# Routing one chunk ahead in the experts stage, a rebuilt phase scan, and new first instructions in six kinds of stage

## What is computed

```
phi = k_val[..., None] * theta
num_re = cumsum(p_w * cos(phi)); num_im = cumsum(p_w * sin(phi)); den = cumsum(p_w)
out_re = sum(s_re * qr + s_im * qi)       # s = num / den, summed over the 8 frequencies
```

```
probs = softmax(flat @ router_w); weights, indices = top_k(probs, 2); weights /= weights.sum()
h = silu(flat @ wg) * (flat @ wu) * comb[:, :, None]      # comb: one weight per token and expert
out = shared experts + einsum('tem,emd->td', h, wd)
```

## Time and profile before

| | us |
|---|---|
| median of 3 runs (lowest, highest) | 8263.17 (8258.72, 8267.3) |
| the profiled execution, its own time | 8261.89 |
| its span in the profile | 8260.2 |
| `scan`, 4961 to 5591 | 630 |
| `moe`, 5693 to 6337 | 644 |
| `lru`, 6337 to 6559 | 222 |
| `Aatt`, 282 to 1062 | 780 |
| `Catt`, 3169 to 4388 | 1219 |

### The profile page before, as it was taken

The page is one execution under the profiler, slowest core; times in us unless marked ns, Lnnn a source line. Parts: engine busy times, 40 slices in busy tenths (PEclk is TensorE's granted clock), DMA queues, the critical chain, the costliest instruction groups (busy, mean ns, idle before and its releaser), DMA issues. The chain is left out here.

```text
span 8260.2 us, 122768 instructions
## 1 busy us (share of the span) xinstructions
PE 6734.6 (82%) x30724; PEld 3442.2 (42%) x30724; DVE 4886.6 (59%) x12027; ACT 2733.4 (33%) x6003; POOL 1566.9 (19%) x847
## 2 busy tenths in 40 slices
PE   6799958988898866999994486776886689889989
PEld 3233334554465432222223352334443345544554
DVE  3555557634774535777775749994334676337645
ACT  0255524612471101555551113331110146124621
POOL 1111115100510011000000007880000261006100
PEclk9899979999999987999997698998988899999999
DMA  5322244542454274222223221103001345424541
GB/s 177 95 60 59 52 131 146 172 136 73 149 173 146 81 250 115 72 64 66 64 49 105 82 75 41 30 25 114 23 30 32 101 149 169 139 71 138 172 153 55
DMA packets 921871, 833.01 MB, mean 101 GB/s; under 512 B 239752, under 2 KB 786528, under 8 KB 921248
## 3 DMA queue, kind: packets, MB, share of 16 engines
q1 hardware_dynamic: 491920, 505.95, 21.2%
q10 hardware_dynamic: 429568, 323.08, 12.5%
HBM read 486.33 MB, written 345.74 MB: 101 GB/s over the span
## 5 line engine op out<-in xcount | busy, mean ns | idle before, releaser
L1216 ACT ACTIVATE Catt_E<-Catt_t 128x512 f32<-128x512 f32 x1024 | 576.8, 596 | 501.6 <-DVE Catt_t L1179 319.7
L1155 DVE CUSTOM_DVE_ANT_0 Catt_S<-Catt_s,Catt_win 128x1024 f32<-128x1024 f32 x512 | 621.3, 1215 | 40.9 <-DMA Catt_win<-skewed 38.8
L1155 DVE CUSTOM_DVE_ANT_0 Aatt_S<-Aatt_s,Aatt_win 128x128 f32<-128x128 f32 (+7 forms) x512 | 377.2, 756 | 325.7 <-PE Aatt_s L1094 320.0
L1137 PE MATMUL Catt_o<-Catt_E,Catt_V 128*32 128x256 f32 (+1 forms) x3840 | 548.6, 404 | 0.0
L1216 ACT ACTIVATE Aatt_E<-Aatt_t 128x512 f32<-128x512 f32 (+3 forms) x768 | 355.4, 489 | 325.5 <-PE Aatt_t L1119 257.4
L1179 DVE TENSOR_TENSOR Catt_t<-Catt_t,Catt_near 128x256 f32<-128x256 f32 (+2 forms) x640 | 281.2, 456 | 261.6 <-PE Catt_t L1116 229.9
L1116 PE MATMUL Catt_t<-Catt_Q,Catt_K 123*128 123x512 bf16 x1024 | 327.9, 388 | 91.9 <-ACT Catt_E L1216 71.8
L1094 PE MATMUL Catt_s<-Catt_K,Catt_Q 96*128 96x512 bf16 x1024 | 324.4, 400 | 46.8 <-DMA Catt_near<-near_s 38.1
L2304 PE MATMUL scan_cum<-scan_X,scan_after 128*128 128x512 f32 x448 | 251.3, 644 | 121.8 <-DVE scan_pr L2373 117.5
L1137 PE MATMUL Aatt_o<-Aatt_E,Aatt_V 128*32 128x256 f32 (+2 forms) x2304 | 324.5, 389 | 0.0
L2306 PE MATMUL scan_cum<-scan_X,scan_upto 128*128 128x512 f32 x512 | 279.0, 637 | 39.5 <-POOL scan_X L2280 23.5
(11 more groups left out here) (724 smaller groups left out, 15070.5 us busy)
## 6 DMA issues: line engine op xcount, KB each, us to landing
bias_rows<-line SPq DMA_DIRECT2D x16, 960.0 KB
skewed<-bias_win ACTq DMA_DIRECT2D x16, 960.0 KB, 5.9
Catt_win<-skewed SPq DMA_DIRECT2D x16, 960.0 KB, 4.7
rec<-state_in_r ACTq DMA_DIRECT2D x32, 416.0 KB, 2.4
scan_r<-rec SPq DMA_DIRECT2D x64, 208.0 KB
Aatt_Q<-q_parts SPq DMA_DIRECT2D x32, 384.0 KB
Aatt_K<-k_parts SPq DMA_DIRECT2D x32, 384.0 KB
Catt_Q<-q_parts SPq DMA_DIRECT2D x32, 384.0 KB
```

What stands on the lines that cost most here:

```text
L1137: ins = t.matmul(o_ps[f:f + 2 * hd, x:y], V[:, b, kb, h, :], E[:, kb % NB, h, x:y], start=kb == 0, stop=kb == end and y == hi)
L1155: v.tensor_tensor_reduce(out=S[:, j % 2, 0:w], in0=s_ps[j % 2][:, 0:w], in1=win[:, 0 if causal else h, w0:w0 + w], scale=-1.0, scalar=BIG, ...
L1216: a.activation(E[:, kb % NB, h, lo:hi], t_ps[n % 2][:, 0:hi - lo], ACT.Exp, scale=scale).then_inc(exped, 1)
```

## The change

It does six things.

1. `scan`: `ph` goes to PSUM (one buffer) and so do `ys` (two). The whole number is found by two engines: ACT writes `nn = ph + MAGIC` (a new instruction `whole`), DVE writes `f = (nn - MAGIC) - ph` in one instruction; L2357 on DVE and L2275 on POOL go. PE does the sines before the cosines. POOL's weighing now also waits for DVE's. The lags become 0 to 4.
2. `moe`: the chunk after is routed during this one. The logits of chunk c+1 come after group k = 2, `route` on DVE at k = 3, the exponential on ACT at k = 4, `choose` on DVE at k = 5, the transposes on PE at k = 8, and ACT's copy at k = 9. SP then writes `combT` to memory (`c_s`) and reads it back into `cb` [128, 2, 8, 512], each row broadcast over 64 partitions. The `sel` matmuls go; the second multiply reads `cb` from SBUF. The down product waits group by group.
3. `lru`: the tables are made during `enter`, on DVE and ACT, and kept in SBUF to the end.
4. `qkv_rotary`: PE waits for the weights alone, and the first columns are issued ahead of the table.
5. `thin_attention`: Q and K have their own semaphore and are loaded at once; V, `ext` and `near` count on `late_in`; the first window is loaded right after Q and K, the `of` copies after the second batch; DVE sets the ones in K.
6. `local_attention`: V has its own semaphore `V_in`.

```diff
 # stage_state_scan
+            def whole(it, j):                      # ACT
+                n = it * ST + j
+                a.wait_ge(ph_done, n + 1)
+                a.wait_ge(f_done, n + 1)
+                a.activation(nn[:, j % 2, :], ph[:], ACT.Identity, bias=magic[:]).then_inc(rounded, 1)
-            pipelined(a, B, ST, ((0, trig), (3, store)))
+            pipelined(a, B, ST, ((1, trig), (0, whole), (4, store)))
-                    for i in range(2):
+                    for i in (1, 0):               # PE: sines, then cosines
...
+            def fraction(it, j):                   # DVE
+                n = it * ST + j
+                v.wait_ge(rounded, n + 1)
+                v.wait_ge(trig_done, n + 1)
+                v.scalar_tensor_tensor(out=f[:, j % 2, :], in0=nn[:, j % 2, :], scalar=-MAGIC, in1=ph[:],
+                                       op0=ALU.add, op1=ALU.subtract).then_inc(f_done, 1)
             def phase(it, j):
+                v.drain()
                 v.wait_ge(r_in[j % R], it * (ST // R * 16) + (j // R + 1) * 16)
-                v.wait_ge(f_done, n + 1)
-                v.tensor_tensor(khm(ph[:, j % 2, :]), khm(th[...]), r[...], ALU.mult)
-                v.drain()
-                v.tensor_scalar(nn[:, j % 2, :], ph[:, j % 2, :], MAGIC, -MAGIC, ALU.add, ALU.add).then_inc(ph_done, 1)
+                v.tensor_tensor(khm(ph[:]), khm(th[...]), r[...], ALU.mult).then_inc(ph_done, 1)
-            pipelined(v, B, ST, ((0, phase), (1, weigh), (2, read), (3, reduce)))
+            pipelined(v, B, ST, ((1, fraction), (0, phase), (2, weigh), (3, read), (4, reduce)))
-            pipelined(g, B, ST, ((1, weigh), (0, fraction), (2, add)))
+            pipelined(g, B, ST, ((2, weigh), (3, add)))
             def weigh(it, m):                      # POOL
+                g.wait_ge(x_done[1], it * ST + (m + 3))
 # stage_experts
+            def weights(it, c):                    # SP
+                s = c % 2
+                sp.wait_ge(combT_done, it * 2 + (c + 2))
+                sp.dma_start(c_s[s * NE:(s + 1) * NE, :], combT[:, s, :]).then_inc(c_out[s], 16)
+                sp.wait_ge(c_out[s], it * 16 + (c // 2 * 16 + 32))
+                sp.wait_ge(hid_done, it * (2 * NJ) + (c * NJ - NJ + 2 + NJ))
+                rows = c_s[s * NE:(s + 1) * NE, :].rearrange("(j e) t -> e j t", e=2)
+                for e in range(2):
+                    sp.dma_start(cb[e * 64:(e + 1) * 64, s], rows[e:e + 1].to_broadcast([64, NR, CH])).then_inc(cb_in[s], 16)
+            def chunk(it, c, more, ahead):
+                if more:
+                    columns(it, c, ahead)
+                for u in range(c * 4, c * 4 + 4):
+                    tail.load(sp, it, u)
+                if more:
+                    weights(it, c + 1)
...
-                    if j < NR:                     # PE
-                        if j == 0:
-                            t.wait_ge(combT_done, nc_ + 2)
-                        t.wait_ge(hid_done, n + 2)
-                        t.matmul(c_ps[:], sel[:, j * P:(j + 1) * P], combT[:], start=True, stop=True).then_inc(cb_done, 1)
+                    if more and k == 2:
+                        logits(it, c + 1)
+                    if more and k == 8:
+                        turn_weights(it, c + 1)
...
+            def chunk(it, c, more, ahead):         # PE
+                up(it, c, more, ahead)
+                if ahead:
+                    t.wait_ge(silu_done, it * (2 * NJ) + (c + 1) * NJ)
+                    turn(it, c - 1) if c else turn(it - 1, 1)
+                down(it, c)
+            logits(0, 0)
+            turn_weights(0, 0)
+            chunks(t, chunk)                       # 2 chunks unrolled, a loop over 2 batches, 2 unrolled
+            def chunk(it, c, more, ahead):         # DVE
...
+                    ins = v.tensor_tensor(h, sg[:, k % 2, :], u_ps[k % 2][:], ALU.mult)
+                    if j < NR:
+                        v.drain()
+                        if j == 0:
+                            v.wait_ge(cb_in[c], it * 32 + 32)
+                        ins = v.tensor_tensor(h, h, cb[:, c, j, :], ALU.mult)
+                    ins.then_inc(hid_done, 1)
+                    if more and k == 3:
+                        route(it, c + 1)
+                    if more and k == 5:
+                        choose(it, c + 1)
 # stage_enter, with the recurrence's tables (the same instructions as before, in a class)
+            tables.load(sp, logs)
+            columns(0)
+            tables.sines(s)
+            with s.Fori(1, B) as it:
+                columns(it)
+        @block.vector
+        def _(v):
+            tables.make(v)
 # stage_qkv_rotary
+            columns(0, 0)
+            sp.dma_start(rt[:], rot.rearrange("(t p) a d -> p t a d", p=P)).then_inc(r_in, 16)
...
-            t.wait_ge(w_in, 16 * 8)
+            t.wait_ge(w_in, 16)
-            v.wait_ge(w_in, 16 * 8)
+            v.wait_ge(r_in, 16 * 7)
 # stage_thin_attention
-            sp.wait_ge(set_up, 1)
-            t.wait_ge(set_up, 1)                   # now only ahead of the first turned maxima
-                    t.wait_ge(head_in[b], it * (16 * LOADS) + 16 * LOADS)
+                    t.wait_ge(head_in[b], it * 32 + 32)
-            g.memset(K[K0:K0 + PARTS], 1.0)
-            v.wait_ge(set_up, 1)
+            v.memset(K[K0:K0 + PARTS], 1.0).then_inc(K_ones, 1)
+            if causal:
+                v.wait_ge(win_made, 1)
 # stage_local_attention
-                             ).then_inc(head_in[b], 16)
+                             ).then_inc(V_in[b], 16)
```

More of the change, by code:

```diff
@@ L341, in _, with columns @@
                 s.sem_inc(cols_out[i], 16)
-            with s.Fori(0, B) as it:
+            def columns(it):
                 for u in range(NT):
@@ L1014, in load @@
             def load(it, b):
-                if b == 1 and not causal:
+                if b == 1 and not causal and not isinstance(it, int):
                     window(it, 0)
@@ L1172, in add_near @@
                 b, h, kb = i // GS, i % 2, i % GS // 2
+                if i % GS == 0 and not causal:
+                    v.wait_ge(late_in[b], it * (16 * LATE) + 16 * LATE)
                 for c, lo, hi, n, some in units[i]:
@@ L2323, in trig @@
                 a.activation(ab[:], f[:, s, :], ACT.Abs)
[L2324 removed]
+                a.activation(sn[:, s, :], f[:, s, :], ACT.Sin, scale=-TWO_PI)
                 a.drain()
@@ L2425, in _ @@
             sp.dma_start(wd_sb[:], wd.rearrange("(k p) n -> p k n", p=P)).then_inc(wd_in, 16)
-            with sp.Fori(0, B) as it:
-                for c in range(2):
-                    sp.wait_ge(tail.y_done, it * NT + (c * 4 + 4))
-                    apart(sp, pl.sp_unread)
-                    sp.dma_start(xc[:, c], act_in["cols"].rearrange("(k p) t -> p k t", p=P)[:, :, bass.ds(it * TP + (PAD + c * CH), CH)]
-                                 ).then_inc(x_in[c], 16)
-                for u in range(NT):
-                    tail.load(sp, it, u)
+            weights(0, 0)
+            chunks(sp, chunk)
         @block.gpsimd
@@ L2495, in down @@
                     tail.y_free(t, it, u)
-                    for j in range(NJ):
+                    for k, j in enumerate(order):
+                        if u == c * 4:
+                            t.wait_ge(hid_done, it * (2 * NJ) + (c * NJ + k + 3))
                         ins = t.matmul(tail.y[u % 2][:], hid[:, j, (u % 4) * P:(u % 4 + 1) * P], wd_sb[:, j, :],
-                                       start=j == 0, stop=j == NJ - 1)
+                                       start=k == 0, stop=k == NJ - 1)
                     ins.then_inc(tail.y_done, 1)
-            pipelined(t, B, 2, ((0, up), (0, ready), (1, turn), (0, down)))
+            def chunk(it, c, more, ahead):
+                up(it, c, more, ahead)
+                if ahead:
+                    t.wait_ge(silu_done, it * (2 * NJ) + (c + 1) * NJ)
[4 more added lines that the diff above has]
+            chunks(t, chunk)
+            turn(B - 1, 1)
         @block.scalar
@@ L2523, in store @@
                     tail.store(a, it, u)
-            pipelined(a, B, 2, ((0, up), (1, store)))
+            def chunk(it, c, more, ahead):
+                up(it, c, more)
+                if ahead:
+                    store(it, c - 1) if c else store(it - 1, 1)
+            exp(0, 0)
+            move_weights(0, 0)
+            chunks(a, chunk)
+            store(B - 1, 1)
             tail.finish(a)
@@ L2621, in stage_recurrence @@
+def stage_recurrence(nc, act_in, tables, bre, bim, cre, cim, d, out):
     with ExitStack() as ctx:
@@ L2735, in _ @@
-            v.drain()
-            v.tensor_scalar(n3[:, 0:1], n3[:, 0:1], -MAGIC, None, ALU.add)
-            v.drain()
-            rest = ex[:, 1:2]
-            for part in (6.28125, 0.0019350051879882812, float(2 * np.pi - 6.28125 - 0.0019350051879882812)):
```

(4 more changed lines are left out.)

330 lines of the change are left out of this document (186 added, 144 removed).

## The result

| | before | after |
|---|---|---|
| median, us | 8263.94 (4 runs, 8258.72 to 8267.3) | 7960.99 (4 runs, 7958.03 to 7969.76) |
| the profiled execution's span | 8260.2 | 7957.9 |

The ratio is 0.9636, with a 95% interval of 0.9619 to 0.9652: 303 us less. Forecast were 7973 (7905 to 8035), 290 less.

What follows compares the result with a forecast made beforehand. Serial stages, `scan` bound by DVE and `moe` by PE; gains 106 (scan) + 102 (experts) + 23 (recurrence) - 2.5 (`enter`) + 13 + 25 + 18 + 6 (fronts) = 290.5 off 8261.9, plus 1.3, gave 7973 us, range 7905 to 8035.

## What to carry to other kernels

When a DVE instruction takes longer than its shape, look whether it ends just behind one of POOL's; put one of its two SBUF sources into PSUM, and remember that two such holds in a row are paid once. Price a pause of PE by what follows it too: filling rests of 3.8 us, one in eight steps, with useless matmuls took six slow steps out of `scan` and made it 7 to 10 us shorter. Before a difference of a few us in one stage is called a gain, see how much that stage varies in kernels that leave it alone. When a transfer is added to a queue in program order, work out the ring that it closes (what stands behind it, and what that feeds), not only the room before its first use.

## What the runs showed of the hardware

When DVE's hardware loop jumps back, its next instruction comes 0.2 us later in most stages, but (in the two traces) 5.0 to 6.6 in `Catt`, `H0att`, `H1att` and, after the change, `B1att`. A broadcast of 2 x 1024 KB from 16 KB each in memory, in two DMAs, lands in 10.5 us; 960 KB read plainly land in 4.7, so reading one source 64 times costs about the same per byte. One float32 matmul of 512 columns is two records of 0.43 us at 2.4 GHz. Setting 3 x 8192 bfloat16 ones takes 6.9 us on DVE and on POOL alike.
